# State-space block with read-outs added in pairs on GpSimd, and a division ahead of the maxima in latent attention

## What is computed

```
# state-space block, on the layer-normed x; d_inner 512, 8 states, dt_rank 16
delta, Bm, C = softplus(low @ W_dt + b_dt), low_B, low_C     # low = xc @ W_x, 32 wide
h_n   = exp(delta * A_n) * h_n + delta * Bm_n * xc           # scan over the 112 rows
y     = sum over n of C_n * h_n, + xc * D
out   = (y * silu(z)) @ W_out
...
# latent attention, 16 heads of 8
scores = einsum('bhsk,bhtk->bhst', Q[..., :KPH], K) / sqrt(KPH)
attn   = softmax(scores, axis=-1)
ao     = einsum('bhst,bhtv->bhsv', attn, V)
```

## Time and profile before

| | |
|---|---|
| time, median of 3 runs | 3149.69 us (3149.64 to 3155.45) |
| profiled execution: time / span | 3149.95 us / 3148.2 us |
| busy share of the span: PE, PEld, DVE, ACT, POOL | 87%, 56%, 64%, 48%, 15% |
| from 100 to 820 us (state-space groups), 720 us: PE, DVE, ACT, POOL busy | 617.9, 577.1, 405.0, 35.0 us; granted clock 0.91 |
| from 2480 to 2783 us (latent attention), 303 us: the same | 241.5, 145.8, 90.9, 77.8 us; granted clock 0.94 |
| scan, drive, read-out, each of 64 | 3.88, 2.02, 2.02 us |

### The profile page before, as it was taken

How to read it: one execution, slowest core, us unless ns; L and a number is a source line. 1 busy time by engine, 2 the same in 40 slices (tenths; PEclk the granted TensorE clock), 3 DMA queues, 4 the chain that set the end, 5 groups by cost and what they waited for, 6 DMA issues and landing times. The chain is left out here.

```text
span 3148.2 us, 60127 instructions
## 1 busy us (share of the span) xinstructions
PE 2729.9 (87%) x20702; PEld 1773.1 (56%) x20703; DVE 2000.7 (64%) x4542; ACT 1522.9 (48%) x2982; POOL 464.0 (15%) x482
## 2 busy tenths in 40 slices
PE   7788888996789999999876689999999887869994
PEld 3344444443456766677765357777776544456662
DVE  2588888888557777777554457777776444563334
ACT  2565656554146666666442146666665233202222
POOL 0000000000210000000033110100100122224441
PEclk9899999997989999999877789999999899969997
DMA  4000000000100000000000100000000300002125
GB/s 109 0 1 0 0 0 0 0 1 0 34 16 20 20 20 20 20 20 15 1 14 1 38 16 20 24 20 20 24 20 6 121 13 14 13 17 64 62 63 162
DMA packets 57937, 80.70 MB, mean 26 GB/s; under 512 B 8880, under 2 KB 47058, under 8 KB 57490
## 3 DMA queue, kind: packets, MB, share of 16 engines
q1 hardware_dynamic: 51778, 62.69, 6.9%
q0 software_dynamic: 6048, 16.52, 1.7%
HBM read 63.59 MB, written 15.60 MB: 25 GB/s over the span
## 5 line engine op out<-in xcount | busy, mean ns | idle before, releaser
L1116 DVE CUSTOM_DVE_ANT_0 xa_h_scores<-xa_h_score_bank,xa_h_added 112x375 f32<-112x375 f32 x1024 | 518.0, 544 | 148.5 <-PE xa_h_score_bank L1051 133.5
L1210 ACT ACTIVATE xa_h_probs<-xa_h_scores,xa_h_negmax 112x375 f32<-112x375 f32 x1024 | 561.4, 600 | 0.9 <-DVE xa_h_negmax L1123 0.6
L1063 PEld LDWEIGHTS xa_h_turn_bank<-keep_ident,xa_h_probs 112*125 112x125 f32 x3072 | 398.8, 190 | 91.2 <-DVE xa_h_probs_t L1130 22.2
L1063 PE MATMUL xa_h_turn_bank<-keep_ident,xa_h_probs 112*125 112x112 f32 x3072 | 438.6, 280 | 8.7 <-DVE xa_h_probs_t L1130 8.5
L1130 DVE COPY xa_h_probs_t<-xa_h_turn_bank 125x448 f32<-125x448 f32 x512 | 319.0, 623 | 150.8 <-PE xa_h_turn_bank L1063 137.5
L1216 ACT ACTIVATE xa_h_probs_t<-xa_h_turn_bank 125x448 f32<-125x448 f32 x256 | 138.6, 541 | 304.5 <-PE xa_h_turn_bank L1063 304.5
L464 PE MATMUL mb_y_bank<-mb_read_out,keep_ident 128*128 128x448 f32 x512 | 231.2, 600 | 25.6 <-DVE mb_read_out L666 25.6
L659 DVE TENSOR_TENSOR_SCAN mb_state<-mb_decay,mb_drive 128x1792 f32<-128x1792 f32 x64 | 248.6, 3884 | 2.1 <-ACT mb_decay L593 2.1
L1051 PE MATMUL xa_h_score_bank<-xa_h_keys,xa_h_queries 32*112 32x375 f32 x2048 | 231.8, 522 | 11.3 <-DVE xa_h_row_max L1116 10.7
L1076 PEld LDWEIGHTS xa_h_sums_bank<-xa_h_probs_t,xa_h_values 125*32 125x32 f32 x6144 | 142.0, 110 | 154.3 <-DVE xa_h_probs_t L1130 149.2
L1076 PE MATMUL xa_h_sums_bank<-xa_h_probs_t,xa_h_values 125*32 125x112 f32 x6144 | 202.7, 265 | 14.6 <-issue 7.0
(11 more groups left out here) (341 smaller groups left out, 4241.6 us busy)
## 6 DMA issues: line engine op xcount, KB each, us to landing
xa_context<-in_ctx_t SPq DMA_DIRECT2D x64, 375.0 KB, 3.1
lm_w<-in_m_w SPq DMA_DIRECT2D x16, 512.0 KB, 9.8
lm_e_wide<-lm_result_rows SPq DMA_DIRECT2D x8, 896.0 KB, 9.2
keep_x<-in_x SPq DMA_DIRECT2D x4, 896.0 KB, 15.4
lm_latent_rows<-lm_rows SPq DMA_DIRECT2D x8, 448.0 KB, 3.2
out_x<-keep_x SPq DMA_DIRECT2D x8, 448.0 KB, 5.9
xa_mask_raw<-in_key_mask SPq DMA_DIRECT2D x1, 1312.5 KB
mb_f_pw<-in_pw SPq DMA_DIRECT2D x1, 1024.0 KB
```

Source lines behind the costliest of these rows:

```text
L1063: last = pe.transpose(turn_bank[(par + kc) % 2][0:KP, g * S:(g + 1) * S], probs[par][:, g, kc * KP:(kc + 1) * KP], keep.ident[0:S, 0:S])
L1116: dve.tensor_tensor_reduce(scores[par][:, g, :], score_bank[g][0:S, 0:SK], added[s][:, :], 1.0, -BIG, ALU.add, ALU.max, row_max[par][:, g: ...
L1210: act.activation(probs[par][:, g, :], scores[par][:, g, :], ACT.Exp, bias=negmax[s][:, G * c + g:G * c + g + 1]).then_inc(probs_ready, 1)
```

## The change

Three edits. (1) GpSimd adds the read-outs of states 2k and 2k + 1 into the second buffer (`add_pair`, four a group), and TensorE adds only the sum to the accumulators, at the end of the odd states; `pair_ready` stands between them. The read-out of an even state now waits for `pair_ready`, that of an odd one for `summed`. (2) `cast_parts` becomes `cast_first`, which runs ahead of `softplus`, and `cast_second`, which runs inside it after its third chunk; VectorE makes `delta` after the last read-out and not before it. (3) In latent attention `divide(t - 3)` stands ahead of both maxima.

```diff
+            def add_pair(g, k):
+
+                pool.wait_ge(read_out_ready, N * g + 2 * k + 2)
+                pool.tensor_tensor(read_out[:, 1, :, :], read_out[:, 0, :, :], read_out[:, 1, :, :], ALU.add).then_inc(pair_ready, 1)
+
             def group(g, at, final=False):
+                for k in range(N // 2 - 1):
+                    add_pair(g, k)
                 if not final:
                     split_low(g + 1)
+                add_pair(g, N // 2 - 1)
...
             def add_state(g, n):
-                pe.wait_ge(read_out_ready, N * g + n + 1)
+
+                k = n // 2
+                pe.wait_ge(pair_ready, N // 2 * g + k + 1)
                 for c in range(IC):
-                    last = pe.matmul(y_bank[c][:, 0:T], keep.ident[:, :], read_out[:, n % 2, c, :], start=False, stop=n == N - 1)
+                    last = pe.matmul(y_bank[c][:, 0:T], keep.ident[:, :], read_out[:, 1, c, :], start=False, stop=n == N - 1)
                 last.then_inc(summed, 1)
...
-                    add_state(g, n)
+                    if n % 2 == 1:
+                        add_state(g, n)
...
                     bank = front(g, DELTAS + m)
                     act.activation(above[:, m, :], bank[:, 0:T], ACT.Relu, bias=b_dt[:, m:m + 1])
                     act.activation(soft[:, m, :], bank[:, 0:T], ACT.Abs, bias=b_dt[:, m:m + 1]).then_inc(front_read[(DELTAS + m) % 2], 1)
+                    if m == 2:
+                        cast_second(g)
...
                     if n == 6:
+                        cast_first(g)
                         softplus(g)
-                        cast_parts(g)
...
-                reuse(dve, summed, N * g + n - 1)
+                reuse(dve, summed if n % 2 else pair_ready, N // 2 * g + n // 2)
...
                     if n + 1 < N:
                         make_drive(g, n + 1)
-                    elif not final:
-                        make_delta(g + 1)
                     make_read_out(g, n)
                 if not final:
+                    make_delta(g + 1)
                     make_drive(g + 1, 0)
...
-                if has(t):
-                    find_max(t, 0)
                 if has(t - 3):
                     divide(t - 3, 1 - par)
                 if has(t):
+                    find_max(t, 0)
                     find_max(t, 1)
```

More of the change, by code:

```diff
@@ L332, in mamba_groups @@
             sem(n) for n in ("decay_ready", "drive_ready", "state_ready", "read_out_ready", "summed"))
+        pair_ready = sem("pair_ready")
         skipped, gated, x_added = sem("skipped"), sem("gated"), sem("x_added")
@@ L558, in read_low, with cast_first @@
                 act.activation(low[:, :], row_bank[0][:, 0:T], ACT.Copy).then_inc(row_read[0], 1)
-            def cast_parts(g):
+            def cast_first(g):
                 for k in range(2):
@@ L565, in cast_parts, with cast_second @@
                 act.activation(low_parts[:, :], low[0:3 * LOW, :], ACT.Copy).then_inc(parts_cast, 1)
+            def cast_second(g):
                 act.wait_ge(split, 2 * (g + 1) + 1)
@@ L631, in _ @@
             read_low(-1)
+            cast_first(-1)
             softplus(-1)
-            cast_parts(-1)
             normalise_rows(1)
@@ L669, in finish @@
             def finish(g):
-                dve.wait_ge(summed, N * (g + 1))
+                dve.wait_ge(summed, N // 2 * (g + 1))
                 dve.wait_ge(front_read[(GATES + 2) % 2], used(g, GATES + 2) + 1)
```

## The result

| | before | after |
|---|---|---|
| time, median | 3152.57 us (3149.64 to 3156.1, 4 runs) | 3242.03 us (3237.7 to 3244.25, 4 runs) |
| ratio, 95% interval | | 1.0282 [1.0263, 1.0301] |
| span of the profiled execution | 3148.2 us | 3235.9 us |
| granted clock, mean | 0.922 | 0.899 |

The change makes the kernel 2.8% slower: 3242 us, as forecast, and well outside the noise.

A forecast was written before the change was run, and what follows sets the result against it. TensorE was taken to bound states 2 to 5 of a state-space group, VectorE right behind. Seven groups +112, last group +23.9, prologue casts -3.7, latent attention -38: +94 on 3149.95 us gave 3244 us, range 3180 to 3285.

The forecast's parts named there:

- (a): In a pair of states, GpSimd's addition waits for VectorE's scan of the even state to end: 3.88 us.
- rival in which the scan doesn't exclude GpSimd: State-space additions run beside the scan: 3151 us, or 3108 us if the clock then holds; chance 0.11.
- (b): In a pair, GpSimd's addition of two read-outs itself takes 3.98 us; bounds 3.06 and 4.11.
- (c): In a pair, TensorE sees the end of GpSimd's addition 0.15 us later.
- (g): TensorE's additions, after about 7 us of idling, run at a low clock: 1.8 us more; bounds nothing and 3.0.
- (d): TensorE's wait for the pair holds up the next odd state's spreading; from additions to VectorE's drive 3.97 us.
- (e): In a pair, VectorE's drive and read-out of the even state take 3.88 us.
- (f): In a pair, VectorE's scan, drive and read-out of the odd state take 7.65 us.
- rival for all of them: TensorE's state-space additions run wholly at half speed: 24 x 1.2 us more, 3273 us; chance 0.06.
- head and the end of a group: Scan 0 to scan 2 15.3 us (-2.0); end 13.8 to state 7's drive, then 25.1 (+5.0).
- last group: State-space group without convolution: scan 2 to gated_y takes 83.9 us instead of 60.0, +23.9.
- casts in the prologue: Both casts and ACT's 2.51 us of waiting for GpSimd leave the path behind the logarithm: -3.7 us.

The follow-up runs named there:

- memset: Changed kernel with GpSimd writing same-size zeros to an unread buffer instead of each addition, even states left out of the sum: 3035.8 us, ratio 0.9642.
- fill: Changed kernel with two of the four convolution banks of each group computed twice on TensorE: 3208.27 us, ratio 1.0184 to the kernel before.
- latent_only: Kernel before with only the latent-attention edit (division ahead of the first maximum): 3106.96 us, ratio 0.9863.
- pairs_only: Kernel before with only the GpSimd additions of pairs, delta staying ahead of the last read-out: 3320.54 us, ratio 1.054.
- defer: Changed kernel with TensorE adding each pair's sum one state later, behind the spreading for the next odd state: 3085.4 us, ratio 0.9794 to the kernel before.
- single: Changed kernel with GpSimd multiplying the odd read-out by 1.0 into an unread buffer instead of adding, even states left out: 3271.43 us, ratio 1.0376.
- double: Changed kernel with GpSimd making each addition twice, first into an unread buffer: 3383.51 us, ratio 1.0734 to the kernel before.
- one_pair: Kernel before with moved casts, latent edit, TensorE's additions behind the spreading; GpSimd adds only states 2 and 3, accumulated after state 4: 3041.56 us, ratio 0.9654.

## Why the prediction was right

The time came out at the forecast (3242.03 against 3244), and the mechanism was the one described; the terms came out as follows.

- **(a) GpSimd waits for the scan.** Right: 3.72 us of waiting in each inner pair. The rival in which the scan doesn't exclude GpSimd is excluded by the 7.47 us rows, and `memset` shows what it would have looked like.
- **(b) The addition, 3.98.** One of them, at 936.53, meets an idle VectorE and takes 3.96; behind a wait it takes 3.75, as if the 0.2 us of its start-up were spent while waiting.

```profile
936.53 3.96 POOL L388 TENSOR_TENSOR mb_read_out<-mb_read_out 128x1792 f32<-128x1792 f32 x1 [16.36 <-DVE mb_read_out L683]
```

- **(c) The hand-over, 0.15.** It was 0.06.
- **(a) to (c) together** were forecast at 8.0 and took 7.7 (0.16 + 3.72 + 3.75 + 0.06); the 0.3 too much made up for 0.3 too little in (g) of the first pair, which is why that pair came out at 25.29 to the forecast's 25.3. That is luck.
- **(d), (e), (f).** Right to 0.1. The whole pair is 0.16 + 3.72 + 3.75 + 0.06 + 6.07 (additions to drive, 3.97 and 2.1 of clock) + 3.87 + 7.66 = 25.29.
- **(g) The clock, 1.8.** The right mechanism, shown by `fill`, but the term was undersized: 2.1, 3.1 and 1.9 us in the three places of a group. The second one ran wholly at the lower level, which I had priced at 3.0 as the bound and given as a rival for all of them. That is why the second pair takes 26.28 and not 25.3, and most of the 6 us by which the seven groups came out longer than 112.
- **The head and the end of a group.** 15.30 and 13.57 + 25.37 = 38.94 us; forecast 15.3 and 13.8 + 25.1 = 38.9.
- **The last group,** +24.3 (from its first scan) against +23.9; with the 2 us by which this group differs between traces of the same code, no more than agreement within that.
- **The casts in the prologue,** -4.7 against -3.7.
- **Latent attention,** -42.2 against -38: the gain a step was larger than 1.31. Of the 31 steps between the first and the last product, 22 got 1.4 to 1.6 us shorter, three 1.3, the last three not at all, and the other three 6.8 together, which I have not traced. The rival in which nothing is gained there is excluded by `latent_only`.
- **The unchanged stages,** -7.8 us, were taken as zero. This stretch is 3 to 8 us shorter than in the kernel before in the traces of all eight kernels in which GpSimd has additional instructions in the state-space block (`pairs_only`, `defer`, `fill`, `memset`, `single`, `double` and `one_pair` besides the changed one), and within 2 us of it in those of the five without. The granted clock in the first 100 us of the stretch is 0.88 after against 0.86 before, and in the last 100 us 0.85 against 0.80; but `defer` and `memset`, shorter by 4.6 and 4.7 us, have 0.78 in the last 100. Where the difference comes from stays open.

So the overestimate of the unchanged and the latent stages (12 us) and the underestimate of the groups (5 us net of the prologue) partly cancel; the agreement within 2 us is luck, the one within some 10 is not. Two of the announced signs were wrongly worked out though the sum had them right: VectorE's idle time before the odd drives had to be (a) to (d) and (g) less the scan, 13.8 - 3.9 = 9.9, not 8; and two waits for `heads_t` of 1.4 us stay, both at the end of the loop (2864.74 and 2868.63) and both there before, where I wrote none above 0.3.

What the prediction lacked is how the cost divides. It priced one chain of 25.3 us per pair. `defer` shows that 3.74 us of it are VectorE's blocking, which stays wherever TensorE waits, and that the rest, the wait for the scan, the low clock and the additions of TensorE themselves, lay on the path only because `spread` was queued behind them.

## What to carry to other kernels

Before work is given to an idle engine, look at which instruction stands behind the new wait on the engine that receives the result: here one call moved by one state is worth 157 us, and it decides the sign. Read GpSimd's time beside a busy VectorE as its own time plus what is left of VectorE's current two-operand instruction, and add its own time again to VectorE's next one; take that as the usual case and not as a bound, since in `one_pair` a short GpSimd instruction waited out three VectorE instructions (9.00 us, where the same one takes 1.98 in the changed kernel). And when a bound engine gets less work but a longer idle stretch, its next instructions may run at half the clock: price them from a row that stands behind such a stretch.

## What the hardware did that was not expected

- The scan, with two operands in SBUF, excludes GpSimd as the products do and is itself held by it: 7.47 us for an addition of 3.75, 4.75 for a scan of 3.88.
- GpSimd reading a single operand is excluded just as well (8.13 us behind a scan), while a write of the same size passes beside the scan in 1.59 us.
- On GpSimd the multiplication of one operand by a constant (4.5 us behind a wait, 4.73 alone) took longer than the addition of two (3.75 and 3.96), both float32 of 128x1792.
- Who goes first is not settled by the order in which the two ask, as far as rows show it: in `double` the engines took turns, instruction by instruction (5.70, 5.74 and 5.59 us); in `one_pair` GpSimd waited out three VectorE instructions (9.00 us); and a step that starts 0.02 us ahead of a scan took 1.02 us in one kernel and 4.72 in another.
- Useless matmuls made the kernel faster: 3242.03 to 3208.27 us with 16 more matmul passes in each of two pairs of a group.
